# Second cross attention of a four-stage block on one Trainium2 core: VectorE's instructions of two statistics chains laid between independent ones

## The reference

```python
x = x + L0_xattn(ctx, layernorm(x), ...)             # 16 heads of 64, with rmsnorm of q and k
x = x + L0_ffn(layernorm(x), wg, w1, w3, w2)         # 8 experts, top 2
x = x + L1_xattn(layernorm(x), ctx, ctx, mask, ...)  # 16 heads of 8: the stage of this change
x = x + L1_ffn(x_as_tokens, ...)                     # 2 layers: local attention and a gated feed forward

def L1_xattn(q, k, v, mask, w_q, w_k, w_v, w_o):     # D_K = 8, H = 16
    query, key_, value = proj(q, w_q), proj(k, w_k), proj(v, w_v)
    scores = einsum('bhqd,bhkd->bhqk', query, key_) / sqrt(8)
    scores = where(mask == 0, -1e9, scores)
    out = einsum('bhqk,bhkd->bhqd', softmax(scores), value)
    return out.reshape(...) @ w_o.T
```

## Time and profile before

| what | value |
|---|---|
| median of 3 runs | 1612.04 us (1609.6 to 1612.83) |
| profiled execution | 1622.13 us |
| its span on the core | 1619.9 us |
| mean granted TensorE clock | 0.973 of full speed |
| busy share of the span: PE, DVE, ACT, POOL | 90%, 76%, 69%, 56% |

### The profile page before, as it was taken

The page is one execution under the profiler, slowest core; times in us unless marked ns, Lnnn a source line. Parts: engine busy times, 40 slices in busy tenths (PEclk is TensorE's granted clock), DMA queues, the critical chain, the costliest instruction groups (busy, mean ns, idle before and its releaser), DMA issues.

```text
span 1619.9 us, 37516 instructions
## 1 busy us (share of the span) xinstructions
PE 1460.8 (90%) x11740; PEld 1196.8 (74%) x11803; DVE 1229.3 (76%) x3032; ACT 1110.5 (69%) x2666; POOL 908.2 (56%) x789
## 2 busy tenths in 40 slices
PE   4899999999988998888887899999898899999988
PEld 3677777777766776666665788888776788888866
DVE  6888888888755556888886788888666787777765
ACT  4888778877754556777774787787723778778732
POOL 4667778777731113444433777777401777777500
PEclk9999999999998997999998999999999999999999
DMA  9800000000012321210000000000000000000000
GB/s 380 325 1 8 11 10 10 11 11 17 13 53 69 87 79 28 62 39 22 22 19 9 13 15 15 15 14 16 10 11 5 5 17 14 15 15 14 11 24 34
DMA packets 87336, 62.62 MB, mean 39 GB/s; under 512 B 52037, under 2 KB 72901, under 8 KB 86469
## 3 DMA queue, kind: packets, MB, share of 16 engines
q1 hardware_dynamic: 83141, 53.00, 10.5%
q0 software_dynamic: 4096, 8.40, 1.8%
HBM read 21.30 MB, written 30.41 MB: 32 GB/s over the span
## 4 chain that ended last, share of the span: by engine, by line
PE 53%; DVE 27%; ACT 9%; issue 6%; POOL 3%; DMA 1%; DVEq 0%; another core or an unknown queue 0%; SPq 0%; POOLq 0%; ACTq 0%
PE slot L1685 6%; PE slot L461 5%; PE slot L463 4%; PE slot L462 4%; PE slot L1668 4%; PE slot L1629 4%; PE slot L1703 3%; PE slot L1638 3%; ACT a_p L743 3%; DVE a_sum L861 3%; PE slot L1938 2%; POOL a_rq L1106 2%; DVE a_ssq L971 2%; PE slot L1679 2%; PE slot L1189 2%
## 5 line engine op out<-in xcount | busy, mean ns | idle before, releaser
L1045 POOL TENSOR_TENSOR rs<-mv,nhalf 128x1 f32 (+1 forms) x160 | 96.6, 604 | 240.2 <-DVE mv L1040 175.1
L1854 POOL TENSOR_TENSOR d_A<-d_A,d_B 128x1024 f32<-128x1024 f32 x64 | 150.8, 2356 | 134.0 <-DVE d_B L1792 133.8
L1858 POOL TENSOR_TENSOR d_r<-d_vv,nhalf 128x16 f32<-128x16 f32 x64 | 186.5, 2914 | 47.5 <-DVE d_vv L1814 46.9
L743 ACT ACTIVATE d_p<-slot,d_nm,d_r 128x128 f32<-128x128 f32 x512 | 185.6, 468 | 27.2 <-DVE d_nm L1805 27.2
L743 ACT ACTIVATE a_p<-slot,a_nm,a_rq 128x77 f32<-128x77 f32 x512 | 163.7, 432 | 56.5 <-DVE a_nm L768 56.5
L743 ACT ACTIVATE c_p<-slot,c_nm 128x77 f32<-128x77 f32 x512 | 116.9, 359 | 30.2 <-DVE c_nm L1477 30.2
L1685 PE MATMUL slot<-d_v,d_pT 128*128 128x65 f32 x1024 | 121.8, 272 | 1.7 <-ACT d_pT L1722 1.7
L1685 PEld LDWEIGHTS slot<-d_v,d_pT 128*128 128x128 f32 x1024 | 119.4, 192 | 2.4 <-ACT d_pT L1722 2.1
L750 POOL TENSOR_TENSOR a_p<-a_p,a_rc 128x616 f32<-128x616 f32 x64 | 80.0, 1250 | 71.5 <-DVE a_rc L863 70.9
L1773 DVE TENSOR_TENSOR d_A<-slot,T 128x1024 f32<-128x1024 f32 x64 | 78.3, 1224 | 45.6 <-PE slot L1629 45.5
L1801 DVE TENSOR_REDUCE slot<-slot 128x8 f32<-128x1024 f32 x64 | 78.9, 1233 | 28.1 <-PE slot L1668 25.5
(11 more groups left out here) (288 smaller groups left out, 4495.2 us busy)
## 6 DMA issues: line engine op xcount, KB each, us to landing
routed<-zero SPq DMA_DIRECT2D x2, 9216.0 KB, 48.6
b_x<-routed SPq DMA_DIRECT2D x80, 64.0 KB
answers<-b_y SPq DMA_DIRECT2D x40, 128.0 KB
X<-in_x SPq DMA_DIRECT2D x2, 1024.0 KB, 8.1
d_zx<-Z SPq DMA_DIRECT2D x64, 32.0 KB
H<-Z SPq DMA_DIRECT2D x64, 32.0 KB
out<-f_o SPq DMA_DIRECT2D x8, 256.0 KB, 2.0
d_zx<-Z SPq DMA_DIRECT2D x64, 31.8 KB
```

Of the source, the lines that this page charges most:

```text
L743: i = e.activation(t["p"][:, h, :], R[slot][:, k // nbank, nk * (k % nbank):nk * (k % nbank) + nk], ACT.Exp, bias=t["nm"][:, h:h + 1], sca ...
L1045: return e.tensor_tensor(rs[:, bass.ds(b, 1)], mv[:, bass.ds(b, 1), 1:2].rearrange("p a b -> p (a b)"), nhalf[:, 0:1], ALU.pow)
L1854: e.tensor_tensor(t["A"][:, p, :], t["A"][:, p, :], t["B"][:, p, :], ALU.add).then_inc(S("d_key"), 1)
L1858: e.tensor_tensor(t["r"][:, it.m(2, 4), :], t["vv"][:, p, :], nhalf[:, 0:16], ALU.pow).then_inc(S("d_key"), 1)
```

## The change

In `c_vector` nothing is added or taken away: the same instructions with the same semaphores stand in another order. The first chain's BN_STATS, BN_AGGR and `mv` move behind `c_qTl`, `c_kl` and `c_kbl`. In the second group the add into `X` moves ahead of the reciprocal, BN_STATS behind the reciprocal, and BN_AGGR stays behind `c_xT`.

```diff
-                    e.wait_ge(S("c_mix"), count(b, 2, 2))
-                    apart(e)
-                    e.bn_stats(st[:, 1, :], rows(X, b)).then_inc(S("c_st"), 1)
-                    e.wait_ge(S("c_st"), count(b, 1, 3))
-                    apart(e)
-                    e.bn_aggr(agg[:, 1, :], st[:, 1, :]).then_inc(S("c_st"), 1)
-                    e.wait_ge(S("c_st"), count(b, 2, 3))
-                    e.tensor_tensor(rows(mv, b), agg[:, 1:2, :], eps[:, 1:2, :], ALU.add).then_inc(S("c_st"), 1)
+                b1 = b
                 b = it.b(3)
                 if b is not None:
                     e.wait_ge(S("ac_v"), count(b, base=NB))
                     e.scalar_tensor_tensor(out=t["qT"][1][:, it.m(3, 2), :], in0=R[0][:, 0, 0:128], scalar=float(DH1) ** -0.5,
                                            in1=t["qT"][0][:, it.m(3, 2), :].bitcast(F32), op0=ALU.mult, op1=ALU.subtract)\
                         .then_inc(S("c_sp"), 1)
+                if b1 is not None:
+                    e.wait_ge(S("c_mix"), count(b1, 2, 2))
+                    apart(e)
+                    e.bn_stats(st[:, 1, :], rows(X, b1)).then_inc(S("c_st"), 1)
+                if b is not None:
                     e.tensor_tensor(t["kl"][:], R[0][:, 0, 128:128 + SK], t["kh"][:].bitcast(F32), ALU.subtract)\
                         .then_inc(S("c_sp"), 1)
+                if b1 is not None:
+                    e.wait_ge(S("c_st"), count(b1, 1, 3))
+                    apart(e)
+                    e.bn_aggr(agg[:, 1, :], st[:, 1, :]).then_inc(S("c_st"), 1)
...
                     e.wait_ge(S("c_sp"), count(b, 2, 3))
                     e.tensor_tensor(t["kb"][1][:, it.m(3, 2), :, :], t["kl"][:].unsqueeze(1).to_broadcast([128, 4, SK]),
                                     blocks, ALU.mult).then_inc(S("c_sp"), 1)
+                if b1 is not None:
+                    e.wait_ge(S("c_st"), count(b1, 2, 3))
+                    e.tensor_tensor(rows(mv, b1), agg[:, 1:2, :], eps[:, 1:2, :], ALU.add).then_inc(S("c_st"), 1)
...
+                if b4 is not None:
+                    e.tensor_tensor(rows(X, b4), rows(X, b4), R[0][:, 1:2, 256:384], ALU.add).then_inc(S("ac_add"), 1)
                 if b3 is not None:
                     e.wait_ge(S("ac_PV"), count(b3, base=NB))
                     e.reciprocal(t["rcT"][:], R[0][:, 1, 384:512]).then_inc(S("c_rcT"), 1)
+                if b4 is not None:
+                    e.wait_ge(S("ac_add"), count(b4, base=NB))
+                    apart(e)
+                    e.bn_stats(st[:, 0, :], rows(X, b4)).then_inc(S("ac_bn"), 1)
+                if b3 is not None:
                     e.wait_ge(S("c_rcT"), count(b3))
                     e.tensor_tensor(t["oT"][:, it.m(5, 2), :], R[0][:, 1, 0:128], t["rcT"][:], ALU.mult).then_inc(S("ac_oTe"), 1)
                 if b0 is not None:
                     e.wait_ge(S("ac_xTp"), count(b0, base=NB))
                     e.tensor_copy(t["xT"][:, it.m(2, 2), :], R[0][:, 1, 128:256]).then_inc(S("ac_xh"), 1)
-                if b4 is not None:
-                    e.tensor_tensor(rows(X, b4), rows(X, b4), R[0][:, 1:2, 256:384], ALU.add).then_inc(S("ac_add"), 1)
-                if b4 is not None:
-                    e.wait_ge(S("ac_add"), count(b4, base=NB))
-                    apart(e)
-                    e.bn_stats(st[:, 0, :], rows(X, b4)).then_inc(S("ac_bn"), 1)
                     stats_tail(e, b4, S("ac_bn"), S("ac_ag"), S("ac_ve"), base=NB)
```

More of the change, by code:

```diff
@@ L1511, in body @@
                         .then_inc(S("c_sp"), 1)
+                if b1 is not None:
[3 more added lines that the diff above has]
+                if b is not None:
                     e.tensor_tensor(t["kl"][:], R[0][:, 0, 128:128 + SK], t["kh"][:].bitcast(F32), ALU.subtract)\
                         .then_inc(S("c_sp"), 1)
+                if b1 is not None:
+                    e.wait_ge(S("c_st"), count(b1, 1, 3))
+                    apart(e)
+                    e.bn_aggr(agg[:, 1, :], st[:, 1, :]).then_inc(S("c_st"), 1)
+                if b is not None:
+                    e.tensor_tensor(t["kb"][0][:, it.m(3, 2), :, :], t["kh"][:].bitcast(F32).unsqueeze(1).to_broadcast([128, 4, SK]),
+                                    head[:].unsqueeze(2).to_broadcast([128, 4, SK]), ALU.mult)
+                if b is not None:
                     blocks = head[:].unsqueeze(2).to_broadcast([128, 4, SK])
-                    e.tensor_tensor(t["kb"][0][:, it.m(3, 2), :, :], t["kh"][:].bitcast(F32).unsqueeze(1).to_broadcast([128, 4, SK]),
-                                    blocks, ALU.mult)
                     e.wait_ge(S("c_sp"), count(b, 2, 3))
```

## The result

| kernel | median of 5 runs | lowest to highest | ratio to before, 95% interval |
|---|---|---|---|
| before | 1611.71 us | 1609.05 to 1612.83 | |
| after | 1599.92 us | 1596.78 to 1602.24 | 0.9936 [0.9922, 0.9951] |

The change takes 11.8 us off. The forecast had the sign and half of the size: 5.5 us, 1606.5, and its range ended 1.6 us above the measured time.

The account below looks back on a forecast made before the run. A ring of waits through several engines, 3.23 + 3.99 = 7.22 us a step, was taken to bound the kernel. 3.6 + 2.5 - 0.6 = 5.5 us off 1612.0 gave 1606.5, own range 1602 to 1608.5, wider range 1601.5 to 1615.

Parts of the forecast that it names:

- The ring of two arcs: Each step is a ring of waits: `c_nm` to `c_qTl` 3.23 us, then `c_qTl` to next `c_nm` 3.99, together 7.22.
- The first arc: From `c_nm` to `c_qTl`, 3.23 us, set by ScalarE, with the first chain of statistics lying inside it.
- Together 3.86 against 3.99: 0.13 per step, 28 steps, 3.6 us: VectorE from `c_qTl` to the next `c_nm` takes 3.86 us instead of 3.99, gaining 3.6 us over 28 steps.
- The group: VectorE's work on the PSUM bank, from the add to the next `c_nm`: 2.25 us instead of 2.81, 0.56 shorter.
- The front part: VectorE from `c_qTl` to the add: 1.61 us, where the reciprocal stood at 1.18, so 0.43 longer.
- The bound of 6.2: Upper bound of the 3.6 us gain: BN_AGGR's stall filled wholly, 0.22 a step, 6.2 us.
- The waits term, 2.5 us,: The reciprocal's waits, remote 2.8 us and for PE's output projection 3.5, total 6.3; 40% gained, 2.5 us.
- The 0.6 us taken off: Loss of 0.6 us where VectorE's second maximum waits for PE's second-half scores in steps at the lower clock.
- Filling the holes: Independent instructions fill idle time between dependent VectorE neighbours, which start 0.43 and 0.44 apart, independent ones 0.20 and 0.21.
- not filled: Rival, chance 0.06: 0.43 and 0.44 are any neighbour's cost, reciprocal to `c_nm` stays 2.81; +12 us, 1624.
- PE becomes the ring: Rival, chance 0.11: `c_kbl` 0.4 late makes second-half scores late for the second maximum; +4 us, 1616.
- the cover of 0.07 to 0.43: Spare time in us between PE's second-half scores being ready and VectorE's second maximum wanting them.

Follow-up runs that it names:

- before again: The kernel before, unchanged, profiled once more in a single execution: 1609.46 us.
- first chain alone: Before with only the first chain of statistics moved behind and between `c_qTl`, `c_kl`, `c_kbh` and `c_kbl`, reciprocal's group in its old order: 1624.68 us, ratio 1.0095.
- group alone: Before with only the add moved ahead of the reciprocal and BN_STATS behind it, first chain left ahead of `c_qTl`: 1587.13 us, ratio 0.9854.

## Why the forecast was right in sign and wrong in size

**The ring of two arcs** was right. The first arc stayed at 3.24, the second got shorter, and the time followed: a clean step went from 7.25 to 6.94 (7.45 to 7.20 in the loop), and the stage from 214.2 to 205.1, which is 9.1 of the 9.5 us between before again and after. That the first arc has no price and the second has one is shown from both sides: the same chain is free ahead of `c_qTl` and costs 12.8 us behind it.

**"Together 3.86 against 3.99: 0.13 per step, 28 steps, 3.6 us" is the step that failed.** Both parts were mis-sized in the same direction. The group was to take 2.25 and takes 2.13 to 2.14: BN_STATS behind the reciprocal costs its neighbour 0.15 and not 0.21, the reciprocal with its neighbour 0.87, `c_oT` to `c_xT` and `c_xT` to BN_AGGR 0.19 each, BN_AGGR to `mv` 0.21. The front part was to end at 1.61 and ends at 1.57: `c_kbh` 0.36 and not 0.39, BN_STATS 0.20. The group so gave 0.68 and not 0.56, the front took 0.38 (1.57 - 1.19) and not 0.43. A clean arc of before is 4.01, of after 3.70: 0.31 a step, 8.7 us if all 28 were clean and written out. The bound of 6.2 that I gave this term allowed only for BN_AGGR's stall and not for the few hundredths at each of eight places; they all fell to one side. What the runs show in its place is 0.31 in the 20 written-out steps and 0.25 in the eight of the loop, 8.2 us and not 3.6.

**The waits term, 2.5 us,** stood on one execution that was 10.1 us above the median. Before again has 2.6 us in 3 waits for the projection, and after has 1.6 in 2: 1.0 gained. The recorded execution of before was 12.7 us above its like, and I had set the sum against it and carried the difference to the median, which was sound for the stage's work and not for its waits.

**The 0.6 us taken off** for the second maximum, which would wait for PE's scores in steps at the lower clock, was right in sign and size: it waits 0.6 us in 2 times in before again and 1.3 in 3 in after. 8.2 + 1.0 - 0.7 is 8.5, against 9.1 in the stage, 9.5 between the two profiled executions and 11.8 between medians. What of the last 2 us is scatter is not settled; the intervals are about 2.4 us to either side. The stage's mean clock was 0.97 in after and 0.95 in before again, two stretches at the lower clock and three; one execution of each doesn't show that the change did this.

**Filling the holes** works: BN_STATS starts 0.20 behind `c_qTl` or `c_xT`, 0.43 behind the add that it depends on, and behind the reciprocal, 0.95 long, after 0.87. The Trainium skill, VectorE: DVE Perf Modes, section "The DRAIN you can't avoid", as the prediction reads it, would have had the group at its old length; the runs don't agree, for neighbours that wait for each other's result. That reading took only half of the section: it also says that a next operation that is not held starts earlier, and independent neighbours here do start 0.20 apart for durations of 0.28. The rival *not filled* is out: it had 1624 for a kernel that takes 1599.92, and 2.81 for a group that takes 2.13.

**PE becomes the ring** is out as well for the change: the second maximum waited 1.3 us in 3 times. PE's waits for `c_kbl` went from 22.2 to 23.9 us, so that its step has as much room as before, though `c_kbl` ends 0.3 later behind `c_qTl`. The low end of the cover of 0.07 to 0.43 is what was there: in the step shown PE's last score of the second half ends at 721.52 and the second maximum starts at 721.57. It is used up at steps of 6.5 us, where the second maximum comes up to 0.1 late, and at 6.4 it waits 0.3. In the first chain alone PE does become the ring, in the steps at and behind the lower clock, for 13.6 us.

**What I did not see** is that the change holds two edits of opposite sign. I had the front part's +0.43 and the group's -0.56 side by side and took them as one move. Times 28 they were +12 and -16 us; measured alone, +15.2 and -22.3. By my own table the group alone was to be forecast at 16 us, and that is what should have been said first.

## What to carry to other kernels

Find the arcs of the ring before moving work: in these kernels an instruction with its stalls was free in an arc that another engine sets, and cost its length in one that its own engine sets, however well it was interleaved there. Where a change has several moves, price and time each alone; here leaving one half out doubles the gain, and one further `mv` moved makes it 1579.7, 2% below before. A producer that is put off needs its consumer put off too where the consumer's engine works in order: the same edit was worth -7.6 us with it and +19.6 without it.

## What the runs showed of the hardware

- Behind the reciprocal, BN_STATS of 128x128 lasts 0.23 us and its independent neighbour starts 0.15 after it; behind `c_qTl` it is 0.28 and 0.20. It reads `X` from SBUF in each.
- Neighbours on VectorE of about 128x128 start 0.20 to 0.21 apart when independent, and 0.43 to 0.45 when the second waits for the first.
- A product of two SBUF operands (`c_kbl`, 128x308) lasts 0.47 us with nothing of GpSimd's beside it, as in each step of after. With `rs` or the copy `c_c` beside it, it lasts 0.47 to 0.62, mostly longer where `rs` starts within 0.06 us of its own start; at 0.55 the next instruction on VectorE starts 0.08 later. Which overlap makes it longer isn't settled.
- The granted clock of a stage follows how PE's work lies in it: 0.87 where the step was 7.6 us with PE waiting for `c_kbl`, 0.98 at the same clean step with the gap filled by needless matmuls, which made the kernel 6.3 us faster. Full speed is 2.4 GHz; in the stages of these two kernels the stretches below it ran at 1.2. The lower clock reached the time through VectorE's waits for PE, 13.6 us against 0.8.
- Two executions of before, 12.7 us apart, differ by 5.8 us in this stage, with nine waits for something remote in the one and none in the other. A single profile doesn't tell which waits are typical.
